# Decoder block on one core: cross-attention weights parked in the first turn and split a slot sooner, cross queries a slot sooner, last layer norms shared between three engines

## What is computed

```python
x = layernorm(x + self_attn(x, Wq, Wk, Wv, Wo))      # 16 heads of 32, 4 key heads, causal
x = layernorm(x + cross_attn(x, ctx, Wq, Wkv, Wout)) # 16 heads, causal mask, ctx is 256 x 128 per sequence
# ffn:
h = (cos(ph) + sin(ph)) * amp                        # amp = sigmoid(x@amp_w+b), ph = pi*tanh(x@ph_w+b)
for l in range(2):
    h = layer_norm(h + (h @ ent_w[l] + ent_b[l]) @ ent_pw[l] + ent_pb[l], ln3_g[l], ln3_b[l])
    h = layer_norm(h + sum_p (h @ path_w[l,p] + path_b[l,p]) * (cos(phase)+sin(phase))[l,p], ln4_g[l], ln4_b[l])
x = layernorm(x + h)
```

## Time and profile before

| | us |
|---|---|
| median of 3 runs (968.82 to 972.22) | 972.0 |
| the profiled execution, its own time | 972.42 |
| its span | 970.6 |
| PE busy | 890.3 (92%) |
| DVE busy | 682.1 (70%) |
| ACT busy | 543.3 (56%) |
| POOL busy | 500.6 (52%) |

### The profile page before, as it was taken

The page is one execution under the profiler, slowest core; times in us unless marked ns, Lnnn a source line. Parts: engine busy times, 40 slices in busy tenths (PEclk is TensorE's granted clock), DMA queues, the critical chain, the costliest instruction groups (busy, mean ns, idle before and its releaser), DMA issues. The chain is left out here.

```text
span 970.6 us, 19586 instructions
## 1 busy us (share of the span) xinstructions
PE 890.3 (92%) x5892; PEld 741.8 (76%) x5892; DVE 682.1 (70%) x2071; ACT 543.3 (56%) x1658; POOL 500.6 (52%) x793
## 2 busy tenths in 40 slices
PE   4989999999859999999999998769999999999893
PEld 4878888888748788888888887457778778778672
DVE  4668888888947877787777776436666756657457
ACT  3655556655635676565657546337555555564361
POOL 0356454566654545554654523511763764665466
PEclk9889999999979999999999999779999999999997
DMA  4554434444663766475475436271002002001001
GB/s 145 169 194 147 159 117 170 143 144 163 196 210 122 215 186 190 145 250 141 147 226 156 147 109 216 83 282 45 1 1 87 1 1 87 1 1 44 1 1 44
DMA packets 79075, 118.53 MB, mean 122 GB/s; under 512 B 7920, under 2 KB 41744, under 8 KB 78224
## 3 DMA queue, kind: packets, MB, share of 16 engines
q1 hardware_dynamic: 75552, 113.85, 36.1%
q10 hardware_dynamic: 3440, 3.67, 1.2%
HBM read 58.76 MB, written 17.83 MB: 79 GB/s over the span
## 5 line engine op out<-in xcount | busy, mean ns | idle before, releaser
L958 ACT ACTIVATE prob<-bank,nmax 128x128 f32<-128x128 f32 (+1 forms) x512 | 209.5, 433 | 25.1 <-DVE nmax L1090 22.7
L161 PE MATMUL bank<-w_ffn,hT 128*128 128x512 f32 x768 | 194.6, 405 | 0.0
L1090 DVE CUSTOM_DVE_ANT_0 bank<-bank,mask 128x128 f32<-128x128 f32 (+1 forms) x512 | 168.0, 385 | 4.1 <-PE bank L1278 3.5
L161 PEld LDWEIGHTS bank<-w_ffn,hT 128*128 128x128 f32 x768 | 142.9, 191 | 31.4
L1292 PE MATMUL bank<-ident,prob 128*128 128x128 f32 x768 | 121.6, 282 | 17.4 <-ACT probT L971 11.0
L161 PE MATMUL bank<-xT,w_att 128*128 128x256 f32 x864 | 120.9, 294 | 11.8 <-DVE w_att L999 11.8
L807 POOL TENSOR_TENSOR zone<-raw,zone 128x256 fp32r<-128x256 f32 x128 | 95.7, 780 | 64.8 <-ACT zone L928 64.8
L161 PEld LDWEIGHTS bank<-xT,w_att 128*128 128x128 f32 x864 | 115.5, 199 | 15.5 <-DVE xT L1078 9.7
L971 ACT ACTIVATE probT<-bank 128x512 f32<-128x512 f32 x97 | 58.5, 603 | 108.7 <-PE bank L1317 107.3
L1278 PE MATMUL bank<-k,q 96*128 96x128 f32 (+1 forms) x512 | 100.9, 300 | 11.4 <-DMA q<-stage 11.4
L958 ACT ACTIVATION_READ_ACCUMULATOR prob<-bank,nmax 128x1 f32 x512 | 111.3, 217 | 0.0
(11 more groups left out here) (118 smaller groups left out, 1513.1 us busy)
## 6 DMA issues: line engine op xcount, KB each, us to landing
q<-stage SPq DMA_DIRECT2D x192, 128.0 KB, 2.3
k<-kstage SPq DMA_DIRECT2D x48, 256.0 KB, 3.6
x<-xres SPq DMA_DIRECT2D x16, 512.0 KB, 4.2
raw<-in_ent_wT SPq DMA_DIRECT2D x32, 256.0 KB, 3.8
raw<-in_ent_pw SPq DMA_DIRECT2D x32, 256.0 KB, 4.4
raw<-in_path_w SPq DMA_DIRECT2D x8, 512.0 KB, 3.6
xres<-in_x SPq DMA_DIRECT2D x8, 512.0 KB, 4.1
xres<-x SPq DMA_DIRECT2D x8, 512.0 KB, 4.8
```

The costliest lines, as they stand in the source:

```text
L161: ins = t.matmul(out, lhs(a, k), rhs(b, k), start=first and n == 0 and m == 0, stop=last and n == len(kts) - 1 and m == 2, skip_group_chec ...
L958: ins = s.activation(prob[:, u, c * width:(c + 1) * width], banks[u][:, c * width:(c + 1) * width], ACT.Exp, scale=-1.0, bias=nmax[:, i % ...
L1090: ins = v.tensor_tensor_reduce(scored, scored, mask[:, S - width:S], scale=-1.0, scalar=3e38, op0=ALU.add, op1=ALU.min, accum_out=nmax[:, ...
```

## The change

It has three parts.

1. *Attention.* Pieces 2 to 5 of the cross weights get places that are free once the self weights are split, and ACT's DMA queue loads them at the end of `first`. In `last_self` they are split a slot or more sooner; sq3, wo0, wo1, cq0, sp0 and sp1 move a slot sooner, sp2 moves to `first_cross`; `path` moves from step 2 to 1, the second `path_bias` from step 1 to 2, and its result is stored behind the folded path. Product j = 2 borrows a transpose bank in place of j = 3, and j = 4 does so only in slots of seven and more.
2. *FFN, first block.* All four folded matrices go through `w_raw`; the second two are loaded when the first two are split, and split one piece per unit inside the first block. POOL adds the identity to the fourth after its second rstd.
3. *FFN, block ends.* The gain is applied together with the mean by DVE (`centre`), so that rstd and residual follow in one instruction (`finish`), and both move into the last units. In the last block POOL adds the residual of two of the four units after ACT has scaled them, and ACT does the final normalisation of all four.

```diff
@@ Turn.fillers, own == "self"
-            out[1] += [("sq", 3)]
+            out[1 if after == "self" else 0] += [("sq", 3)]
...
-                out[1] += [("x1t", 0), ("x1t", 1)]
-                out[2] += [("wo", 0), ("ck", 0)]
-                out[3] += [("cq", 0), ("wo", 1), ("cq", 1), ("ck", 1), ("sp", 0), ("sp", 1), ("sp", 2)]
+                out[1] += [("x1t", 0), ("x1t", 1), ("wo", 0)]
+                out[2] += [("wo", 1), ("cq", 0), ("ck", 0), ("sp", 0), ("sp", 1)]
+                out[3] += [("cq", 1), ("ck", 1)]
         elif own == "cross" and after:
-            out[0] += [U, U, ("cq", 2), U] if wo != "wo" else [("cq", 2), ("cq", 3), U, U]
+            out[0] += [U, U, ("cq", 2), U] if wo != "wo" else [("cq", 2), ("cq", 3), ("sp", 2), U, U]
@@ Turn.borrowed
-        if n < 3 or not self.own or j not in (1, 3, 4):
+        if n < 3 or not self.own or (self.own == "self" and self.after == "cross" and i == 2):
             return None
-        return O_BANK if j == 1 else T_BANKS[(UNITS_OF_STEP * (i - 1) + (1 if j == 3 else 2)) % 2]
+        unit = {2: 1 if n > 3 else None, 4: 2 if n > 6 else None}.get(j)
+        return O_BANK if j == 1 else unit and T_BANKS[(UNITS_OF_STEP * (i - 1) + unit) % 2]
@@ split_at, t is last_self
-            return {(0, False): (OUTPUTS, C_KEYS), (1, False): (C_KEYS, C_KEYS + 2), (2, False): (C_KEYS + 2, C_QUERIES),
-                    (3, True): (C_QUERIES, C_VALUES)}.get((i, early), (0, 0))
+            return {(0, False): (OUTPUTS, C_KEYS + 1), (1, True): (C_KEYS + 1, C_KEYS + 3), (1, False): (C_KEYS + 3, C_QUERIES),
+                    (2, True): (C_QUERIES, C_VALUES)}.get((i, early), (0, 0))
@@ SP, sp 0
                                 store_path(t)
+                                for l in range(NL):
+                                    wait_alone(q, s_pbm, 2 * l + 2, s_passed)
+                                    q.dma_start(A["fd"][l, 1][:, KT, :], acc[:, NP * l, :]).then_inc(s_pbst, 16)
                                 wait_alone(q, s_pst, 16 * B, s_passed)
@@ POOL, attention
-                    if t.own == "self" and i == (2 if t is last_self else 3):
+                    if t is last_self and i in (0, 2):
+                        path_bias(i // 2)
+                    if t.own == "self" and i == (1 if t is last_self else 3):
                         path()
-                    if t is last_self and i < NL:
-                        path_bias(i)
@@ ACT, attention, end of a turn
+                if t is first:
+                    wait_alone(s, s_wlo, OUTPUTS, s_passed)
+                    for n in range(PARKED_FREE, PARKED):
+                        home, s_home, _ = piece_home(n)
+                        s.dma_start(home, piece_of(n)).then_inc(s_home, 16)
@@ ffn_phase
-    stage_raw = [w_raw[:, 0, :, :], w_raw[:, 1, :, :], y[:, :, :], ht[:, :, :, :].rearrange("p h k j -> p h (k j)")]
+    stage_raw = [w_raw[:, n % 2, :, :] for n in range(2 * NL)]
...
+                if n >= 2:
+                    wait_alone(q, s_wlo, KT * (n - 1), s_passed)
@@ POOL, FFN, order of a block
+                for n, u in enumerate(norms[b]):
+                    if 2 <= n < UN - 2 and not (last and n == UN - BT + 1):
+                        lo(n - 2)
                     rstd_of(u)
+                    if last and UN - BT <= u < UN - BT + BY_GPSIMD:
+                        if u == UN - BT:
+                            lo(u - 1)
+                        add_residual(u - (UN - BT))
+                    if last and u >= UN:
+                        shift_of(u - UN)
+                    if n < BT:
+                        residual(n)
+                    if b == 0 and n == 1:
+                        residual_of_path(1)
@@ ACT, FFN
-            stage_hi(2)
-            stage_hi(3)
-            s.wait_ge(s_wlo, 2 * NL * KT)
...
+                        if b == 0 and n < 2 * KT:
+                            piece_hi(2 * KT + n)
...
+                    for i in range(BY_GPSIMD):
+                        s.wait_ge(s_rstd, b * LN + number[b][UN - BT + i])
+                        s.wait_ge(s_cen, b * BT + (i + 1))
+                        s.activation(y[:, i, :], y[:, i, :], ACT.Copy, scale=rstd[:, i, 1:2]).then_inc(s_scaled, 1)
+                    for i in range(BT):
+                        s.wait_ge(s_shift, i + 1)
+                        s.activation(y[:, i, :], y[:, i, :], ACT.Identity, bias=centres[:, i:i + 1], scale=rstd[:, i, 1:2]).then_inc(s_fin, 1)
@@ DVE, FFN, finish
+                    if last and i < BY_GPSIMD:
+                        wait_alone(v, s_sum, n, s_passed)
+                        statistics(UN + i)
+                        return
...
+                    v.scalar_tensor_tensor(y[:, i, :], y[:, i, :], rstd[:, i, 1:2], xb[b % 2][:, i, :], ALU.mult, ALU.add).then_inc(s_sum, 1)
```

More of the change, by code:

```diff
@@ L682, in between @@
                     if i == 2 and t is first:
-                        load_piece(0)
-                        load_piece(1)
+                        for n in range(PARKED_FREE):
+                            load_piece(n)
                         q.dma_start(acc[:, :, :], A["path_b"].rearrange("l w d -> (l w d)").partition_broadcast(P).rearrange("p (n d) -> p n d", d=D)).then_inc(s_pb, 16)
@@ L689, in between @@
                         load_path(t)
-                        wait_alone(q, s_pbm, 2, s_passed)
-                        load_piece(4)
-                        load_piece(5)
                     if t is last_self and i == 1:
-                        for l in range(NL):
-                            wait_alone(q, s_pbm, 2 * l + 2, s_passed)
-                            q.dma_start(A["fd"][l, 1][:, KT, :], acc[:, NP * l, :]).then_inc(s_pbst, 16)
                         wait_alone(q, s_xs, B, s_passed)
@@ L919, in row_hi @@
                 if row == 0:
-                    s.wait_ge(s_wlo, OUTPUTS)
-                if row == 2:
                     s.wait_ge(s_wlo, OUTPUTS + PARKED)
+                if row == 3:
                     s.wait_ge(s_pc, B)
+                    s.wait_ge(s_pbm, 2 * NL)
                 if row >= 4 and row % 2 == 0:
@@ L1418, in ffn_phase @@
     LN = UN + BT
-    NORMS = list(range(UN - 1)) + [UN, UN - 1] + [UN + i for i in range(1, BT)]
-    number = {u: n + 1 for n, u in enumerate(NORMS)}
+    NORMS = list(range(UN - BT + 1)) + [u for i in range(BT - 1) for u in (UN + i, UN - BT + i + 1)] + [UN + BT - 1]
+    LAST_NORMS = list(range(UN - BT + 2)) + [u for i in range(BT - 2) for u in (UN + i, UN - BT + i + 2)] + [UN + BT - 2, UN + BT - 1]
+    norms = [NORMS] * (NB - 1) + [LAST_NORMS]
+    number = [{u: n + 1 for n, u in enumerate(order)} for order in norms]
+    BY_GPSIMD = BT // 2
     plan_pro = Plan(full, drained)
@@ L1490, in _, with residual_of_path @@
             g.wait_ge(s_c, 4)
-            for l in range(NL):
+            def residual_of_path(l):
                 g.wait_ge(s_wraw[2 * l + 1], 16)
@@ L1683, in unit, with centre @@
                     k.drain(("mm", u), v.tensor_tensor(y[:, i, :], banks[plan.bank(("mm", u))][:, :], bias[:, s_, :], ALU.add))
-                    if u >= 1:
+                    if u > UN - BT:
+                        if not last:
+                            finish(u - 1 - (UN - BT))
+                    elif u >= 1:
                         normalise(u - 1, s_norm)
+                    if u > UN - BT + 1 and not last:
+                        normalise(UN + u - 2 - (UN - BT), s_fin)
                     k.wait_drained(("mm", u))
                     statistics(u)
+                    if u >= UN - BT:
+                        centre(u)
+                    if u > UN - BT and last:
+                        finish(u - 1 - (UN - BT))
+                def centre(u):
+                    i = u % BT
+                    v.wait_ge(s_agg, b * LN + number[b][u])
+                    v.scalar_tensor_tensor(y[:, i, :], y[:, i, :], mv[:, i, 0:1], lng[:, :], ALU.subtract, ALU.mult).then_inc(s_cen, 1)
                 def finish(i):
                     n = b * BT + (i + 1)
-                    v.wait_ge(s_g, n)
+                    if last and i < BY_GPSIMD:
+                        wait_alone(v, s_sum, n, s_passed)
+                        statistics(UN + i)
+                        return
+                    v.wait_ge(s_rstd, b * LN + number[b][UN - BT + i])
                     v.wait_ge(s_res, n)
-                    v.tensor_tensor(y[:, i, :], y[:, i, :], xb[b % 2][:, i, :], ALU.add).then_inc(s_sum, 1)
+                    v.wait_ge(s_cen, n)
+                    v.scalar_tensor_tensor(y[:, i, :], y[:, i, :], rstd[:, i, 1:2], xb[b % 2][:, i, :], ALU.mult, ALU.add).then_inc(s_sum, 1)
                     v.wait_ge(s_sum, n)
@@ L1699, in body @@
                     if kind == "mm":
-                        if n == UN - 1:
-                            finish(0)
                         unit(n)
+                        if b == 0 and 3 <= n <= 2 * KT + 2:
+                            piece_lo(2 * KT + n - 3)
```

(13 more changed lines are left out.)

83 lines of the change are left out of this document (37 added, 46 removed).

## The result

The changed kernel takes 963.0 us (median of five runs, 961.0 to 964.7) against 972.0 (five runs, 968.7 to 972.7): a ratio of 0.992, interval 0.990 to 0.995. That is 9 us less, where 15 were forecast. A second measurement later (`changed_again`) gave 0.988 (0.985 to 0.991), a gain of 12 us. One execution in all the runs, of `row4_early`, was in a slow state (3271 us) and is left out.

The account below looks back on a forecast made before the run. PE, 92% busy, was taken to bound the kernel, with DVE the bound in last_self. Terms: 972.42 - 10.0 + 1.0 - 2.9 - 2.0 - 1.5 = 957.0 us; range 950.5 to 964.0.

Parts of the forecast that it names:

- last_self and first_cross, -10.0: End of self, start of cross attention: row 2 and path moved, DVE's 9.50 us wait goes; 10.0 us less.
- rival (a): SP's wait for the path's store to land only changes place, before the second queries: +3.8 us, 960.8; chance 0.13.
- First turn, +1.0: First attention turn: ACT's 1 MB of pieces delays its load of the next xT; 1.0 us more, ends 0 and 5.1.
- Borrowed banks, -2.9: Cross turns: six 0.48 us waits of the transposes for DVE's drain of a borrowed bank go; 2.9 us less.
- Rival (e): Cross turns: ordinary banks drained late in each of 28 slots, adding 19.3 us, 979.2, slower than before; chance 0.03.
- First FFN block, -2.0: FFN start: drain 2.9 us sooner, PE's clock kept (1.4), against POOL's identity (1.8) and DVE's splits (0.5); 2.0 us less.
- Block ends, 0: Ends of FFN blocks 1 to 3: DVE's work moves into units 13 to 15, hidden behind 96 gate products; no change.
- Last block, -1.5: Last FFN block: last normalisation ends at 966.6, not 968.12; 1.5 us less, ends -3.5 and +1.1.
- the pessimistic end: Last block: POOL's two additions each hold one DVE instruction for 1.30 us; block 1.1 us slower than before.
- Rival (c): Last block gains nothing from sharing, as DVE and POOL block each other: +2.6 us, 959.6; chance 0.10.
- no wait of DVE or ACT on a raw row in `first_cross`: Sign of being right: in first_cross neither engine waits for a raw row any more; before, 9.50 and 10.55 us.
- PE's wait over 3 us for queries in the second turn: Sign of being wrong: PE waits over 3 us for stacked queries in the second turn (or in first_cross).

Follow-up runs that it names:

- row4_early: Changed kernel, but SP loads raw row 4 at the end of last_self, ahead of the store of its output: 963.6 us, ratio 0.993 to the kernel before.
- row4_xres_early: Changed kernel with raw row 4 loaded at the end of last_self and xres at the start of first_cross, ahead of the query copies: 957.0 us, ratio 0.987.
- ffn_alone: The kernel before with only the new FFN phase: ratio 0.997 to the kernel before (0.995 to 0.999).
- pieces_late_only: Changed kernel, but ACT loads the four parked pieces at the start of last_self, not the end of first: 961.5 us, ratio 0.988 to the kernel before.
- last_cross_pieces_first: Changed kernel with row 4 and xres early in first_cross, and xres and six gate pieces ahead of last_cross's queries; parked pieces in first: 960.4 us, ratio 0.990.

## Why the prediction was right and wrong

The forecast was 957.0; the direction was right, the size was not: 15 us against 9 (12 in the second measurement).

- **last_self and first_cross, -10.0: the step that failed.** The size of what was removed was right: DVE's 9.50, and 9.5 us had come back at 292.4 in the changed profile (9.6 in the second one). The error is in taking DVE's wait, "the size of the gain", as the net gain of the stretch: I costed what the moved row brings to ACT and DVE and not what stands on SP. SP stores x 7.2 us after DVE has ended it, since the path's store and landing and the rows now stand ahead, waits 5.2 us for the landing (277.46 to 283.33), copies six queries for 3.90, and only then loads rows 4 and 5 and xres. The landing (4.6) and the copies (4.10) were there before; they had cost nothing, since PE came later. Without the stall xres is the next late thing, and 7.0 us went back. Net -2.5 (-4.5 in the second profile). The mechanism is that of rival (a), a late load on SP's queue, at another place and nearly twice its 3.8; that rival looked only at the queries, whose wait did not come. `row4_xres_early` shows the cause: two loads moved, 7.0 becomes 0.2, and the stretch gives 8.0 of the 10.0.
- **First turn, +1.0:** neither shown nor excluded; -0.3 in this profile, 1.6 between the means with and without the pieces, less than the spread. Nor can the runs tell it from the whole 2.9 us that the prediction drew from the Trainium skill (DMA: Bandwidth & Descriptors, Issuing engines are not separate DMA queues). The trace agrees with that page on the sharing itself: four loads issued by ACT lengthened the landing of SP's store from 3.3 to 7.7 us.
- **Borrowed banks, -2.9: mis-sized, it is -4.9.** Of this, 0.7 falls behind the last slot of `first_cross`, where a wait of 1.35 us for `kstage` (at 327.16) became one of 0.7. In a cross turn the gap of 0.48 was worth 0.64, since the profile shows a gap only from the modelled end of the matmul before. Before, from scores to transposes, it was 1.04 us (463.29 to 464.33 of the earlier trace rows); now 0.40:

```profile
463.29 0.56 PE L1278 MATMUL bank<-k,q 96*128 96x128 f32 x4
```
```profile
457.74 0.56 PE L1279 MATMUL bank<-k,q 96*128 96x128 f32 x4
457.94 0.69 DVE L1055 TENSOR_TENSOR xb<-bank,xb 128x512 f32<-128x512 f32 x1 [0.48 <-PE bank L161]
...
458.14 0.62 PE L1293 MATMUL bank<-ident,prob 128*128 128x128 f32 x4
```

The drain comes as late as ever; PE doesn't wait for it. The rest, some 0.1 a turn, stays open. Rival (e) is out.
- **First FFN block, -2.0:** -2.6 in this pair (613.1 to 753.5), -1.7 in `ffn_alone`, -1.7 to -3.4 in all. The transposes wait 0.76, not 3.37, and PE keeps its clock behind them (3.05 for 12 products); POOL's identity takes 1.89 (1.8 expected), of which PE sees one wait of 0.74:

```profile
669.79 0.66 PE L1810 MATMUL bank<-ident,y 128*128 128x128 f32 x4 [0.76 <-DVE y L1702]
670.20 3.05 PE L161 MATMUL bank<-w_ffn,hT 128*128 128x512 f32 x12
...
672.96 1.89 POOL L1504 TENSOR_TENSOR w_raw<-w_raw,ident 128x128 f32<-128x128 f32 x4
...
676.15 1.66 PE L161 MATMUL bank<-w_ffn,hT 128*128 128x512 f32 x6 [0.74 <-POOL hT L1521]
```

- **Block ends, 0:** +0.4.
- **Last block, -1.5:** -1.7. The last drain comes 1.0 us later after the mark at 905.2 (53.0 against 52.0 us; 1.2 was written out), and from there to the last normalisation it takes 8.24 us (956.69 - 948.45) against 8.3 expected. In five profiles, `ffn_alone` and `changed_again` among them, the stretch gives 2.7 to 2.9: PE's clock stays at 1.00 behind the first gates of the last block (900 to 905 in `changed_again`), where in this one it falls to 0.66. The kernel before has the same fall (0.67 at 910 to 915), so 1.2 us here go by the clock. DVE waited 1.30 once for POOL's result, and its own gain took 0.91 at most; the instruction that began second, POOL's addition, was the longer one (1.74 against 1.26). So the blocking of the pessimistic end (1.30 twice) did not come. Rival (c) was right that the sharing does nothing and wrong that it costs 2.6. What is left as the source of the gain is the fused gain and residual and the final pass on ACT; no run parts these.

The profile pair adds up: -0.3, -2.5, -4.9, +0.1 (end of attention), -2.6, +0.4, -1.7 is -11.5, against -11.4; by the medians of the first measurement the gain is 2 us less, within the spread that the first two turns bring. Of the signs named beforehand, the first ("no wait of DVE or ACT on a raw row in `first_cross`") failed, and it pointed near the cause. One sign of being wrong came, PE's wait over 3 us for queries in the second turn (6.83 us), but it could not tell: the kernel before has 5.09 there, and `pieces_late_only`, without the pieces, 6.54. And the earlier trace rows has four dips of the clock, not five; nothing hangs on it.

## What to carry to other kernels

When a stall goes, all that lay under it is next. List what each in-order queue still has to do there, the DMA-issuing one first: what was moved ahead of it, a landing it waits for (here 5.2 us) and copies ahead of a load (3.90) can hold it back while the engines come forward (here by 10.6 us, the load by 2.0). And PE's wait names what came last by the profile, not what is worth mending: with two late loads in a row, mending the one that its wait led to (row 4, through cv) gained nothing alone. Read a change's price stage by stage where one stage has a spread of its own.

## What the runs showed of the hardware

The mark at 78.3 differed by 7.0 us between the eight profiles without the pieces in `first` (-5.7 to +1.3, that of before among them). From there to the first step of `last_self` fifteen of the seventeen profiles took 157.33 to 157.48 us, the other two 157.83 (`ffn_alone`) and 158.23 (`last_cross_pieces_first`). The landing of SP's store of 512 KB took 2.9 to 3.5 us, and 7.7 to 8.2 where ACT's queue had issued 1 MB of loads some 3 us before it. A gap between PE's rows was worth a third more than its figure (0.64 for 0.48).
